# Latent attention with a ternary feed-forward: inputs and keys turned earlier, rope parts in two buffers, two score tiles ahead of the last query product

## The reference

```python
c_kv, c_q = x @ w_dkv, x @ w_dq                  # ranks 64 and 192
k = concat(rope(x @ w_kr) for all heads, c_kv @ w_uk)
q = concat(rope(c_q @ w_qr), c_q @ w_uq)
attn = softmax(q @ k.T / sqrt(64 + 128))
x = layernorm(x + (attn @ (c_kv @ w_uv)) @ w_o)
w1q, w3q, w2q = ternary_quant(w1), ternary_quant(w3), ternary_quant(w2)  # clip(round(w / mean|w|), -1, 1) * mean|w|
out = layernorm(x + (silu(x @ w1q.T) * (x @ w3q.T)) @ w2q.T)
```

## Time and profile before

| | us |
|---|---|
| median of three runs | 900.92 |
| the three runs | 900.05, 900.92, 901.59 |
| the profiled execution | 901.27 |
| its span, first to last instruction | 899.4 |
| PE busy in it | 862.3 (96%) |
| ACT, DVE, POOL busy | 679.5, 677.8, 614.2 |

### The profile page before, as it was taken

One profiled execution on the slowest core, in us unless ns is written; L12 is line 12 of the kernel. 1 busy time (PEld: TensorE's weight loads), 2 busy tenths in 40 slices (PEclk: granted clock), 3 DMA queues, 4 the chain that ended last, 5 costly groups with the idle time before them and its releaser, 6 DMA issues.

```text
span 899.4 us, 17019 instructions
## 1 busy us (share of the span) xinstructions
PE 862.3 (96%) x5188; PEld 503.6 (56%) x5188; DVE 677.8 (75%) x1065; ACT 679.5 (76%) x1095; POOL 614.2 (68%) x436
## 2 busy tenths in 40 slices
PE   9799889999999999999999978999999999999996
PEld 6468534444544445448786834444544445446875
DVE  1779987888888888873567997887888888885366
ACT  3554789999999999990453388999999999996142
POOL 0308867788878888882353887788887888887134
PEclk9899989999999999999999999999999999999999
DMA  9954899999999899996302599999899899999201
GB/s 243 266 204 100 175 201 185 176 184 173 172 185 174 164 177 190 163 183 194 142 1 59 129 190 197 175 179 192 162 175 194 166 172 186 174 169 168 98 1 47
DMA packets 424587, 145.81 MB, mean 162 GB/s; under 512 B 408268, under 2 KB 417184, under 8 KB 423776
## 3 DMA queue, kind: packets, MB, share of 16 engines
q1 hardware_dynamic: 423936, 143.43, 78.7%
q0 software_dynamic: 448, 1.57, 0.5%
q10 hardware_dynamic: 160, 0.26, 0.1%
HBM read 23.85 MB, written 7.60 MB: 35 GB/s over the span
## 4 chain that ended last, share of the span: by engine, by line
PE 73%; DVE 9%; ACT 4%; SPq 4%; POOL 4%; issue 4%; DMA 3%; DVEq 0%; ACTq 0%; POOLq 0%
PE Tb L1268 18%; PE OO L1239 13%; PE Sa L1239 12%; PE Sb L1239 8%; PE Ta L1250 5%; PE Sa L1386 3%; PE Sb L1386 3%; SPq L336 2%; SPq L367 2%; ACT probs L626 1%; DMA PT_dma<-P_parts 1%; PE OO L1416 1%; PE Sb L1278 1%; DVE small L902 1%; POOL turned L446 1%
## 5 line engine op out<-in xcount | busy, mean ns | idle before, releaser
L472 POOL TENSOR_TENSOR P_parts<-probs,P_parts 128x768 f16<-128x768 f32 x256 | 419.9, 1659 | 106.8 <-ACT P_parts L532 106.7
L532 ACT ACTIVATE P_parts<-probs 128x768 f16<-128x768 f32 x256 | 205.7, 842 | 6.9 <-DMA PT_dma<-P_parts 5.6
L926 DVE TENSOR_TENSOR PT_lo<-Ta,PT_hi 128x512 f16<-128x512 f32 x128 | 88.5, 691 | 63.0 <-ACT PT_hi L532 60.8
L902 DVE TENSOR_REDUCE small<-OO 128x1 f32<-128x1024 f32 x96 | 117.1, 1220 | 20.9 <-PE OO L1239 20.8
L1268 PE MATMUL Tb<-PT_dma,V_hi 128*64 128x512 f16 x768 | 132.1, 385 | 0.0
L626 ACT ACTIVATE probs<-OO,small,scales 128x1024 f32<-128x1024 f32 x96 | 115.4, 1202 | 18.0 <-DVE small L905 16.2
L1239 PE MATMUL OO<-K_hi,Q_parts 128*128 128x512 f16 x384 | 116.8, 386 | 9.5 <-ACT probs L626 7.8
L902 DVE TENSOR_REDUCE small<-Sa 128x1 f32<-128x1024 f32 x96 | 116.9, 1218 | 8.9 <-PE Sa L1239 8.9
L626 ACT ACTIVATE probs<-Sa,small,scales 128x1024 f32<-128x1024 f32 x96 | 115.5, 1203 | 4.9 <-DVE small L905 2.7
L1239 PE MATMUL Sa<-K_hi,Q_parts 128*128 128x512 f16 x384 | 115.5, 383 | 2.8 <-ACT probs L626 2.7
L902 DVE TENSOR_REDUCE small<-Sb 128x1 f32<-128x1024 f32 x64 | 77.9, 1217 | 12.0 <-PE Sb L1239 12.0
(11 more groups left out here) (306 smaller groups left out, 1553.0 us busy)
## 6 DMA issues: line engine op xcount, KB each, us to landing
Q_parts<-turned_parts SPq DMA_DIRECT2D x64, 128.0 KB, 2.4
TT<-ternary SPq DMA_DIRECT2D x2, 2304.0 KB, 8.4
Q_parts<-Q_parts SPq DMA_DIRECT2D x16, 256.0 KB, 3.3
PT_dma<-P_parts SPq DMA_TRANSPOSE x256, 3.9
ternary<-tern SPq DMA_DIRECT2D x1, 2304.0 KB, 6.9
xq<-in_L_attn_x_dram SPq DMA_DIRECT2D x2, 1024.0 KB, 10.0
wq_low<-Wq_lo SPq DMA_DIRECT2D x1, 2048.0 KB, 11.3
Wvo_lo<-wvo_low SPq DMA_DIRECT2D x8, 256.0 KB, 4.0
```

Source lines behind the costliest of these rows:

```text
L472: nc.gpsimd.tensor_tensor(P_parts[:, n % DEEP, 1, :], probs[n % DEEP][:, KP * P:S], P_parts[:, n % DEEP, 0, :], ALU.subtract).then_inc(par ...
L532: return nc.scalar.activation(o, i, ACT.Copy, scale=scale)
L902: nc.vector.tensor_reduce(nmax[:, n % 4:n % 4 + 1], scores_bank(n)[:, :], AX.X, ALU.max, negate=True).then_inc(row_max, 1)
L926: nc.vector.tensor_tensor(PT_lo[place].rearrange("p k (t q) -> p t k q", t=2), T_BANK[:, :].rearrange("p (t k q) -> p t k q", t=2, k=KP), ...
```

## The change

**Start, batch 0 alone.** The inputs are turned and the keys projected before the nine ternary turns, on PE and with the copies on ACT that belong to them. The copies of the four rope weight tiles on ACT come behind those of the inputs. The DMAs of `w_qr` (three issues) stand behind those of x and the small weights. DVE's maximum over 4096 columns becomes three parts, two of them earlier, and a small one over the three results.

**Each batch.** A second buffer, `parts_even`, takes the rope parts of even groups, and a half is written again when the moves of the group before last have landed. DVE's low part of half 1 of the group before moves from behind the first latents into the middle of `rotate`, for groups 1 to 3; POOL no longer makes that of group 2. In group 3 tile 2 goes to OO and tile 3 to Ta/Tb. PE runs score tiles 0 and 1, both ahead of tile 3. On DVE and ACT the maximum and the exponent of the first tiles move with that.

```diff
@@ (PE, start)
-            for n in range(9):
-                if n == 0:
-                    pe.wait_ge(ff_scale, 5)
-                turn_ternary(n)
-            pe.wait_ge(ff_sb, 8)
...
                 project((Oa, Ob), lambda kc: wkv[:, kc, :], 1).then_inc(kv_ps, 1)
+                if b == 0:
+                    pe.wait_ge(ff_scale, 5)
+                    for n in range(9):
+                        turn_ternary(n)
@@ (ACT, start)
-            for c in range(4):
-                rotary_high(c // 2, c % 2)
-            for n in range(9):
-                act_.wait_ge(ff_ps, n + 1)
-                copy(tern[:, n * HALF:(n + 1) * HALF], FF[n % 4]).then_inc(ff_sb, 1)
...
                     copy(xT[:, n % 2, n // 2 * HALF:(n // 2 + 1) * HALF], X_BANKS[n]).then_inc(xT_sb, 1)
                 if b == 0:
+                    for c in range(4):
+                        rotary_high(c // 2, c % 2)
+                    for n in range(9):
+                        act_.wait_ge(ff_ps, n + 1)
+                        copy(tern[:, n * HALF:(n + 1) * HALF], FF[n % 4]).then_inc(ff_sb, 1)
                     squares(0)
@@ (rope parts, the same on ACT, POOL and DVE)
+        def parts_of(g):
+            return turned_parts if g % 2 else parts_even
...
-                    if g >= 1:
-                        pool.wait_ge(turned_out[j], b * 64 * GROUPS + 64 * g)
+                    if g >= 2:
+                        pool.wait_ge(turned_out[j], b * 64 * GROUPS + 64 * (g - 1))
@@ (POOL)
                         rotary_parts_low(g, 0)
-                    if g == GROUPS - 2:
-                        rotary_parts_low(g, 1)
@@ (DVE, rotate)
                         if g >= 1:
+                            if j == 2:
+                                rotary_parts_low(g - 1, 1)
                             dve.wait_ge(rope_sum, b * 2 * GROUPS + 2 * g - 1 + dst // 2)
...
                     latents_low(g, 0)
-                    if 0 < g < GROUPS - 1:
-                        rotary_parts_low(g - 1, 1)
+                    if g == GROUPS - 1:
+                        maximum(b * PAIRS * TILES + 1, 1)
                     latents_low(g, 1)
@@ (ACT, group 3)
                     latents_high(g, 0)
-                    latents_high(g, 1)
                     if g == GROUPS - 1:
                         act_.wait_ge(ff_out, 16)
                         exponent(b * PAIRS * TILES, 0)
+                        part_high(b * PAIRS * TILES, 0, None)
+                    latents_high(g, 1)
@@ (PE, group 3)
+                    banks = Q_BANKS[5 - j if g == GROUPS - 1 and j >= 2 else j]
...
                             scores(b * PAIRS * TILES, 0, 0, b * PAIRS * 2)
+                            pe.wait_ge(rope_mul, b * 4 * GROUPS + 4 * GROUPS)
+                            scores(b * PAIRS * TILES + 1, 1, 0, b * PAIRS * 2)
                         query_terms(g, j, range(5))
...
-                pe.wait_ge(rope_mul, b * 4 * GROUPS + 4 * GROUPS)
-                scores(b * PAIRS * TILES + 1, 1, 0, b * PAIRS * 2)
-                pe.wait_ge(lat_lo, b * 4 * GROUPS + 4 * GROUPS)
+                pe.wait_ge(lat_lo, b * 4 * GROUPS + 4 * GROUPS - 2)
                 scores(b * PAIRS * TILES + 2, 2, 0, b * PAIRS * 2)
```

More of the change, by code:

```diff
@@ L312, in _ @@
                         sp.dma_start(wdq_b[:, kc, a, :], w_dq[rows, P:QR]).then_inc(w_in, 16)
+                if b == 0:
+                    sp.dma_start(wqr[:, 0, :], w_qr[0:P, :]).then_inc(w_qr_in, 16)
+                    for i in range(2):
+                        sp.dma_start(wqr[64 * i:64 * i + 64, 1, :], w_qr[P:QR, :]).then_inc(w_qr_in, 16)
                 sp.dma_start(tcos[:, :], cos).then_inc(tables_in, 16)
@@ L628, in exponent, with part_high @@
                                          accum_out=den[:, n // 8 % 2, n // 4 % 2, n % 4:n % 4 + 1]).then_inc(exp_done, 1)
+                def part_high(tile, n, reused):
+                    act_.wait_ge(exp_done, EXP0 + tile + 1)
+                    if reused is not None:
+                        act_.wait_ge(part_in[n % DEEP], reused)
+                    copy(P_parts[:, n % DEEP, 0, :], probs[n % DEEP][:, KP * P:S]).then_inc(part_hi, 1)
                 for g in range(GROUPS):
@@ L680, in _ @@
                 act_.wait_ge(rope_sum, b * 2 * GROUPS + 2 * GROUPS)
+                for j in range(2):
+                    act_.wait_ge(turned_out[j], b * 64 * GROUPS + 64 * (GROUPS - 1))
                 pair_act(0, True, False)
@@ L959, in pair_dve @@
                             rotary_parts_high(GROUPS - 1, n // 2)
+                        if first and n == 0:
+                            for j in range(2):
+                                dve.wait_ge(turned_out[j], b * 64 * GROUPS + 64 * (GROUPS - 1))
                         transposed_low(pair * (TILES // 2) + n // 2, n + 1)
@@ L966, in pair_dve @@
                             reciprocal(pair * 2 + h, h)
-                maximum(b * PAIRS * TILES + 1, 1)
                 maximum(b * PAIRS * TILES + 2, 2)
@@ L1291, in query_terms @@
                         for n in range(2):
-                            last = mm(Q_BANKS[j][n], w, c[:, n * HALF:(n + 1) * HALF], start=(k == 0), stop=(k == 4))
+                            last = mm(banks[n], w, c[:, n * HALF:(n + 1) * HALF], start=(k == 0), stop=(k == 4))
                     if 4 in ks:
@@ L1341, in pair_pe @@
                             next_scores(n + 4)
+                        if first and n == 0:
+                            pe.wait_ge(lat_lo, (b + 1) * 4 * GROUPS)
                         if ahead:
```

52 lines of the change are left out of this document (28 added, 24 removed).

## The result

The changed kernel takes 912.75 us (median of four runs, 912.49 to 913.40) against 900.89: the ratio is 1.0133, with an interval of 1.0117 to 1.0148. It is slower, as forecast, but by 11.9 us where 7.2 were forecast, and beyond the range's upper end of 911.8. The span of its profiled execution is 910.8 against 899.4, 11.4 more.

A forecast was written before the change was run, and what follows sets the result against it. The prediction took the passage from query products to attention as bound by the DVE-ACT chain and what reaches it from POOL and SP. Start 1.15, batches 2.7 and 3.3 added 7.2, giving 908.1 us; range 899.0 to 911.8.

The forecast's parts named there:

- the term for the low parts of group 3: Group 3's rope low parts on DVE: said to cost nothing while SP's moves finish before the first pair's second half.
- The hold in `rotate`: DVE's moved low part is held until POOL's low part ends, lasting 2.1 or more; `rotate(3)` ends 3.4 us later.
- Third exponent: Passage to attention: starts 2.4 us later in batch 0, 2.1 in batch 1, plus 1.65 each for half clock.
- Edits with one answer: Group 3's low parts, other banks and waits ahead of the pairs: cost nothing while SP's moves are done in time.
- What comes back: End of the first pair: a later passage uses up PE's idles, crediting 1.35 us in batch 0, 0.41 in batch 1.
- The start: Before batch 0's query products: row of largest squares 0.5 us sooner, half clock costs 1.65, together +1.15 us.
- The clock term: At the start, PE's projections to latents run at half clock behind an idle of some 3.2 us, costing 1.65.
- (a): Rival: the low part is held in `rotate`, but PE's clock does not fall; 901.4 to 903.2 us, chance 0.20.
- (b): Rival: the low part in `rotate` is not held, batches come to 0; 900.4 to 902.1 us, chance 0.14.
- (c): Rival: low part not held, and time saved on POOL reaches the end; 896.8 us, chance 0.12.
- (d): Rival: half clock as long as in batch 0 at the start and both passages; 911.8 us, chance 0.12.

The follow-up runs named there:

- pool_small: The changed kernel with POOL's low parts of groups 0 to 2 covering 64 of 1024 columns, the rest zero; 910.07 us, single run.
- fill_wait: The changed kernel with 20 identity transposes on PE filling its wait between score tiles 0 and 1; 912.41 us, single run.
- parts_small: The changed kernel with DVE making only 64 of 1024 columns of the first half of group 3's rope parts; 908.02 us, single run.
- wait_moved: low_late with ACT's wait for group 2's moves placed right before its first write to that buffer's memory; 905.96 us, one run.
- low_late: The changed kernel with low parts back behind the first latents and group 2's on POOL; 906.81 us, ratio 1.0056.
- a_wqr_first: The kernel before with the start's part of the change alone, but w_qr's DMAs ahead of x as before; 904.39 us, ratio 1.0024.
- a_only: The kernel before with the start's part of the change alone, w_qr behind x; 905.05 us, ratio 1.0043.
- a_again: The same kernel as a_only, run again beside a_wqr_first on the same chip; 904.17 us, ratio 1.0020.
- order_g1_start: The kernel before with new score-tile order, only group 1 in the second buffer, early inputs and keys, w_qr first, PE filler before the input row; 901.13 us, ratio 1.0008.

## Why the prediction was wrong, step by step

The direction and the mechanism in `rotate` held. What failed is the term for the low parts of group 3: it was put at nothing, and they hold DVE for 1.8 us more in each batch at the sixth exponent, of which 1.5 and 1.2 are left at the ninth.

- **The hold in `rotate`.** Right, though a little shorter than the 2.1 that was to show it. 2.00 from 97.50, ending 1.07 behind POOL's 98.43; `rotate(3)` 3.2 late against the first query product (forecast 3.4). pool_small shows the cause.
- **Third exponent.** Right in sum: +4.3 and +4.1, forecast 2.4 + 1.65 and 2.1 + 1.65. Without half clock it is +2.8 and +2.6 (fill_wait), and the clock is 1.5 and 1.6. That the clock fell here at all is in part luck: in parts_small it did not, in batch 1, behind the same idle of 2.55. And the account was too simple: without the hold in `rotate` and the wait, the new order of the score tiles brings this exponent sooner (wait_moved), and only the late `rotate(3)` turns it into a loss.
- **Edits with one answer.** Here the prediction failed. It said that the low parts of group 3 cost nothing while SP's moves are done. From the third exponent to the sixth it is 8.9, not 7.1: +1.8 in each batch. Part of that returns by the ninth exponent, where the hold on the second half (2.67 before, 1.21 now) is gone; 1.5 and 1.2 stay, 2.7 of the 4.2 us between the forecast 7.2 and the span's 11.4. The prediction had the row that shows such a hold for this line of code, the 2.67, and used it for `rotate` alone; it did not ask which operation of POOL the shifted copy would meet. Its reading that only operations with both inputs in SBUF are held was wrong as well: the copy has one input, and took 2.11. The wait for group 2's moves was in the same sentence, and is 2.6 us of ACT when nothing else is late (low_late). In the changed kernel itself DVE is later still.
- **What comes back.** Near in number, by luck: 6.13 at the sixth exponent becomes 4.84 at the row of sums in batch 0, 1.29 back (forecast 1.35); 5.91 becomes 5.28 in batch 1, 0.63 back (0.41). The forecast credited PE's idles in front of that row. In batch 0 the lateness falls from 5.9 to 4.8 between the ninth exponent and the row, and the idle from 1.35 to 0.41, so some 1.0 came that way. In batch 1 nothing did: the idle stays at 0.42, and the lateness at 5.3 from the ninth exponent on. The rest, 0.3 and 0.6, came back between the sixth and the ninth exponent; the second half's hold that is gone there is the likely reason, but no run shows it by itself.
- **The start.** +0.59, forecast +1.15. The clock term is 8.14 - 6.45 = 1.7, as forecast (1.65), but other executions of the same start lose up to 4.4 by it, above the 2.9 that was given as the bound; the input row came 1.1 sooner, not 0.5.
- **The rivals.** (a) fell: the clock did fall, behind 2.2 and 2.5 us of idle. (b) and (c) fell by the number that was to decide, 2.00. (d) was near in time and wrong in cause: half clock cost 1.5 to 1.7 in the changed kernel, not 2.9; the time went to the second hold.

The sum with the missed term is 7.2 + 2.7 = 9.9, against 11.4. The rest is 0.7 at the third exponents, 0.7 that PE's idles did not give back, 0.7 where nothing was changed, less 0.6 at the start.

## What to carry to other kernels

When a subtraction or a copy between two SBUF tiles is moved, or the work in front of it, look up what GpSimd runs at that moment, for each such operation that shifts and not only for the one that was moved. In these traces the engine that started second was the one held: DVE's copy by 1.4 when POOL was 0.08 ahead, POOL's subtraction by 0.4 when DVE was 0.11 ahead. So a small shift moves a hold from one place to another, and one that goes at one place may come at the next. A new buffer is no free cover: what was a wait for its own last use becomes a wait of whoever owns that memory next.

## What was not expected of the hardware

A copy with a single input in SBUF is held as well: 0.68 alone for 1024 columns, 2.11 while POOL's subtraction ran, and 1.61 for 64 columns. The Trainium skill, on the page "SBUF — State Buffer", section "SBUF: two separate sides", counts DVE operations in a mode that uses both ports among those that take the shared pair; the traces agree by the 2.11 and the 1.61, if the copy ran in such a mode, which no run here shows by itself.

An idle of 2.2 us on PE was followed by half clock (input row, a_wqr_first), where the trace of before had shown this behind 3.15; the cost behind it differs between executions of the same start, 1.7 to 4.4 us. Nor does the same idle always bring it. The 3.15 of the kernel before is there in a_wqr_first too, and full clock follows in both batches, as the 0.60 (1.03 before) shows:

```profile
117.01 0.60 PE L1246 MATMUL OO<-K_hi,Q_parts 128*128 128x512 f16 x2 [3.15 <-ACT probs L625]
```

Its rows of sums come no sooner for that (72.63 and 71.78): half clock behind this idle costs nothing at the end of the pair.

In ten of the traces on the later chips PE waits 0.3 to 2.9 us for `wuv` before 29 us; where it waits 0.6 or more, the input row is later too, by 0.8 to 7.3 against the changed kernel's 53.38. Whether the earlier DMA of x adds to that is not settled: `wuv` was late in traces with `w_qr` behind x (a_only, a_again) and ahead of it (order_g1_start). With the start of before the wait is at most 0.3, in five traces.
